# An expert layer on one core: next rows transposed earlier, bias share formed ahead, y finished by halves, four ranks counted on ScalarE, input check one expert later

## The reference

```python
N = B * S                        # 2048 tokens
k = int(CAPACITY_FACTOR * N / E) # 256 of them for each of 8 experts
xf = x.reshape(N, D)
route_prob = jax.nn.softmax(xf @ Ws + bs, axis=-1).T
route_vals, routes = jax.lax.top_k(route_prob, k)
xin = xf[routes]
h = jax.nn.gelu(jnp.einsum('ekd,edf->ekf', xin, W1) + b1[:, None, :])
out = jnp.einsum('ekf,efd->ekd', h, W2) + b2[:, None, :]
out = out * route_vals[..., None]
final = jnp.zeros((N, D), dtype=x.dtype).at[routes.reshape(-1)].add(out.reshape(-1, D))
```

## Time and profile before

| | us |
|---|---|
| median of 3 runs | 218.7 |
| the runs | 215.75, 218.7, 220.24 |
| the profiled execution, device time | 215.89 |
| its span, first to last instruction | 213.7 |

### The profile page before, as it was taken

How to read it: one execution, slowest core, us unless ns; L and a number is a source line. 1 busy time by engine, 2 the same in 40 slices (tenths; PEclk the granted TensorE clock), 3 DMA queues, 4 the chain that set the end, 5 groups by cost and what they waited for, 6 DMA issues and landing times.

```text
span 213.7 us, 3624 instructions
## 1 busy us (share of the span) xinstructions
PE 184.4 (86%) x1254; PEld 111.5 (52%) x1254; DVE 131.6 (62%) x452; ACT 88.9 (42%) x211; POOL 101.9 (48%) x111
## 2 busy tenths in 40 slices
PE   6888997997999979999999999799879878977970
PEld 2544542444433545367676766333358666865850
DVE  5787879257883898768689788888846311101120
ACT  2423772332722483135643562457535312333320
POOL 0599648000235020820247578500367787888652
PEclk9999999999999999999999999999999999999997
DMA  6625212102100001069910112100022223323123
GB/s 188 186 73 146 77 48 53 40 20 51 31 0 3 0 0 49 2 195 323 317 62 0 52 51 104 52 0 0 15 56 25 38 38 38 44 36 50 25 29 35
DMA packets 16128, 13.64 MB, mean 64 GB/s; under 512 B 3700, under 2 KB 13080, under 8 KB 16104
## 3 DMA queue, kind: packets, MB, share of 16 engines
q1 hardware_dynamic: 12246, 10.61, 16.2%
q0 software_dynamic: 2944, 2.30, 7.7%
q10 hardware_dynamic: 913, 0.43, 0.8%
HBM read 8.02 MB, written 3.21 MB: 53 GB/s over the span
## 4 chain that ended last, share of the span: by engine, by line
PE 41%; DVE 21%; POOL 15%; issue 10%; DMA 6%; ACT 3%; POOLq 1%; DVEq 0%
POOL out L1949 8%; PE psum L1014 7%; DVE mrow L1530 5%; POOL pT L1941 4%; DMA out<-pT,idx 3%; PE psum L911 3%; DVE pT L1676 3%; PE psum L1032 3%; DVE stats L1412 3%; PE psum L921 3%; PE psum L984 2%; PE psum L1095 2%; PE psum L955 2%; PE psum L1051 2%; PE psum L1083 2%
## 5 line engine op out<-in xcount | busy, mean ns | idle before, releaser
L1839 POOL TENSOR_SCALAR ve<-mv 128x4 f32<-128x4 f32 (+1 forms) x19 | 4.4, 231 | 70.3 <-DVE mv L1415 70.2
L780 ACT ACTIVATE pT<-psum 103x512 f32<-103x512 f32 (+1 forms) x36 | 21.2, 596 | 30.2 <-PE psum L986 30.2
L1949 POOL DMA_INDIRECT out<-pT,idx x16 | 25.5, 1594 | 9.7 <-issue 4.2
L911 PE MATMUL psum<-c 128*128 128x512 bf16 x108 | 27.6, 379 | 1.0 <-ACT key_map L805 1.0
L1941 POOL DMA_INDIRECT pT<-gather_rows,idx x16 | 17.7, 1103 | 21.1 <-DVE idx L1730 16.8
L1530 DVE TENSOR_REDUCE mrow<-psum 128x8 bf16<-128x616 f32 x32 | 24.6, 789 | 5.1 <-PE psum L955 5.1
L1741 DVE TENSOR_TENSOR pT<-psum,b_rows 128x256 f32<-128x256 f32 (+1 forms) x10 | 3.7, 371 | 36.2 <-PE psum L1368 36.2
L1356 PE MATMUL psum<-xinT,w 128*128 128x256 f32 (+1 forms) x80 | 16.6, 350 | 4.8 <-ACT xinT L862 4.4
L867 ACT ACTIVATE pT<-psum,b 128x256 f32<-128x256 f32 (+1 forms) x40 | 14.8, 432 | 8.1 <-PE psum L1356 8.1
L1557 DVE RECIPROCAL rden<-psum 128x512 f32<-128x512 f32 (+1 forms) x5 | 13.6, 2716 | 6.7 <-PE psum L1014 6.0
L1368 PE MATMUL psum<-w,pT 128*128 128x128 f32 x128 | 17.4, 284 | 0.2 <-DVE flag L1749 0.2
(11 more groups left out here) (198 smaller groups left out, 374.3 us busy)
## 6 DMA issues: line engine op xcount, KB each, us to landing
w<-in_L_ffn_W SPq DMA_DIRECT2D x16, 256.0 KB, 5.7
gather_rows<-xrow SPq DMA_DIRECT2D x4, 272.0 KB, 2.1
x<-in_x SPq DMA_DIRECT2D x4, 256.0 KB, 4.3
q_stack<-q_hi SPq DMA_DIRECT2D x32, 32.0 KB, 1.8
out<-res SPq DMA_DIRECT2D x4, 256.0 KB, 2.1
q_stack<-q_lo SPq DMA_DIRECT2D x24, 32.0 KB, 1.8
b_rows<-in_L_ffn_b SPq DMA_DIRECT2D x1, 512.0 KB, 3.7
pT<-gather_rows,idx POOLq DMA_INDIRECT x16, 2.6
```

The costliest lines, as they stand in the source:

```text
L780: nc.scalar.activation(pT[0:n, b % 2, s, :], ST_ps[s % 2][0:n, :], ACT.Exp).then_inc(exp_done, 1)
L911: pe.matmul(bank[b][:, :], ident16, c16[:, 0:4 * P], start=True, stop=True)
L1949: nc.gpsimd.indirect_dma_start(flat, bass.IndirectOffsetOnAxis(idx[:, h, e:e + 1], 0), y[:, e, h, :], None, bounds_check=last_row, oob_is_ ...
```

## The change

Five edits, all behind the search:
1. `EARLY = 1`: on PE the transposes of k = 1 stand ahead of y of k = 0.
2. DVE forms b2 times the route value (the bias share) in `y` as soon as the group's rows are transposed, and later, per half, one fused instruction y = psum * route value + share. `y_done` counts halves, and each scatter waits for its own.
3. ACT counts the ranks of experts 4 to 7, second half, with Sign and an accumulator. The sum of signs is mended by half the factor and by an offset in `tile_rows`, which now has a set per half. DVE counts the other four and waits for ACT ahead of the last `idx` write.
4. The check runs on DVE after k = 2, its verdict after k = 3, PE's sum ahead of y of k = 4, in bank 6.
5. A small constant, `slot_mid`, is set on DVE early in the kernel.

```diff
+EARLY = 1
-def group_of(e, h):
-    return [k for k, (of, h0, h1) in enumerate(GROUPS) if of == e and h0 <= h < h1][0]
+def halves_done(n):
+    return n // NG * E * SH + sum(h1 - h0 for _, h0, h1 in GROUPS[:n % NG + 1])
...
-    crow = (own * tile_row[:, None]).astype(np.float16)
+    signed_half = CAP // SH // 2 * J * ((np.arange(SH)[:, None] == SH - 1) & (np.arange(E)[None] >= INDEX_GROUPS[-1][0]))
+    crow = (own[:, None, :] * (tile_row[:, None, None] + signed_half[None])).astype(np.float16)
...
+                (e0, e1), h = INDEX_GROUPS[-1], SH - 1
+                act.wait_ge(idx_ps_done, (again + 1) * len(INDEX_GROUPS))
+                for e in range(e0, e1):
+                    ins = nc.scalar.activation(below[:, e - e0, :], rank_ps[-1][h][:, (e - e0) * P:(e - e0 + 1) * P], ACT.Sign,
+                                               bias=slot_mid[:], scale=-1.0, accum_out=pcount[:, h, e:e + 1])
+                ins.then_inc(act_rank_done, 1)
...
+                    if k + 1 < NG and k < EARLY:
+                        rows_T(again, k + 1)
                     if n >= 2:
-                        pe.wait_ge(y_done, n - 1)
-                    if n == 3:
+                        pe.wait_ge(y_done, halves_done(n - 2))
+                    if n == 4:
                         pe.wait_ge(suspect_done, 1)
...
-                    if k + 1 < NG:
+                    if k + 1 < NG and k >= EARLY:
                         if not again and k >= 2:
                             warm_rows(WARM, (k + 1) % 2)
                         rows_T(again, k + 1)
...
-                                for h in range(h0, h1):
+                                for h in range(h0, h1 - last):
...
+                                signs = last and h == SH - 1
+                                if signs:
+                                    dve.wait_ge(act_rank_done, again + 1)
...
                     for k, (e, h0, h1) in enumerate(GROUPS):
-                        hs, shape = slice(h0, h1), [P, h1 - h0, D]
+                        dve.wait_ge(xinT_ps_done, again * NG + k + 1)
+                        for h in range(h0, h1):
+                            ins = dve.tensor_scalar(y[:, e, h, :], b2_rows[:, e, :], xin[:, e, h, D + e:D + e + 1], None, ALU.mult)
+                        settle(ins)
                         dve.wait_ge(y_ps_done, again * NG + k + 1)
-                        settle(dve.tensor_tensor(y[:, e, hs], bank[6 + k % 2][:, h0 * P:h1 * P].rearrange("p (h d) -> p h d", d=D),
-                                                 b2_rows[:, e, :].unsqueeze(1).broadcast_to(shape), ALU.add))
-                        dve.tensor_tensor(y[:, e, hs], y[:, e, hs], xin[:, e, hs, D + e].unsqueeze(2).broadcast_to(shape),
-                                          ALU.mult).then_inc(y_done, 1)
-                        if not again and k == 1:
+                        for h in range(h0, h1):
+                            dve.scalar_tensor_tensor(y[:, e, h, :], bank[6 + k % 2][:, h * P:(h + 1) * P], xin[:, e, h, D + e:D + e + 1],
+                                                     y[:, e, h, :], ALU.mult, ALU.add).then_inc(y_done, 1)
+                        if not again and k == 2:
                             suspects()
-                        if not again and k == 2:
+                        if not again and k == 3:
                             dve.wait_ge(flag_ps_done, 1)
...
             def scatter(again, e, h):
                 n = again * E + e
-                pool.wait_ge(y_done, again * NG + group_of(e, h) + 1)
+                pool.wait_ge(y_done, n * SH + h + 1)
```

## The result

| | before | changed |
|---|---|---|
| median of 20 runs each, one chip, us | 215.81 | 215.08 |
| lowest and highest | 214.7, 223.89 | 212.95, 218.21 |
| the profiled execution, device time | 215.89 | 214.98 |
| its span | 213.7 | 213.2 |
| its granted clock, mean | 0.993 | 0.983 |

The ratio of the two kernels is 0.9933, with a 95% interval from 0.9905 to 0.9962: 1.45 us less, between 0.8 and 2.05. Both kernels have some executions several microseconds longer; the ratios here leave those out. By 2% the two kernels are the same; by the interval the changed one is the quicker. The forecast was 216.3 and within 2%.

A forecast was written before the change was run, and what follows sets the result against it. POOL, issuing indirect DMAs end to end, was taken as the bound. 1.70 at the front plus 0.64 from gathers gave 2.34 (span 213.7 to 211.4); 218.7 - 2.4 = 216.3 us against the median of three, range 213.2 to 219.2.

The forecast's parts named there:

- POOL as the bound: From 168 to 200 us POOL issues indirect DMAs end to end: 26.26 busy plus 19 gaps of 0.30.
- S(1,0): Scatter-add of expert 1, first half, on POOL: start forecast at 166.22 us in place of 167.94.
- The front, 1.70: POOL's waits for DVE at its first scatters: their removal was to gain 1.70 us by expert 1's first scatter.
- S(0,0): Scatter-add of expert 0, first half, on POOL: start forecast at 159.53 us in place of 160.03.
- S(0,1): Scatter-add of expert 0, second half, on POOL: start forecast at 161.62 us in place of 162.63.
- the moved transposes: On PE, second group's transposes during the first group's Gelu: claimed to add 0.27 us ahead of first group's y.
- ScalarE is late: Rival at the front: slow Signs delay the hidden layer to 156.95; gain 1.7 us, median 217.0; chance 0.10.
- Bias share stops POOL: Rival on DVE's bias products: 13 x 0.337 = 4.4 us lost on POOL, median 220.8; chance 0.13.
- Gathers, 0.64: Second gathers of each pair on POOL: four long ones fall to 1.06 us each, gaining 0.64 in sum.
- The end, 12.8 and rigid: From expert 6's first scatter to span end: 12.8 us set by POOL and landings alone, moving rigidly.

The follow-up runs named there:

- a_again: The changed kernel run again with no edit; median 212.36 us (6 runs), ratio 0.9884 to the kernel before.
- a_tail: The changed kernel with expert 7's first gather moved on POOL behind the scatters of expert 5; median 213.46 us, ratio 0.9871 to the kernel before.
- a_halves_undone: The changed kernel with DVE's two whole-group instructions back, no bias share ahead, y released per group; median 214.93 us, ratio 0.9931 to the kernel before.
- b_again: The kernel before run again, unaltered; median 216.39 us (10 runs), ratio 1.0011 to the kernel before.
- b_wide_rows: The kernel before with only the index constant widened to one set per half, same values; median 218.97 us (2 runs).
- a_share_x4: The changed kernel with each group's bias share formed four times instead of once; 216.48 us (1 run).

## Why the forecast held, and where its steps were off

**POOL as the bound: right.** From S(1,0) to S(5,0) POOL's 0.30 is the only idle time in the changed kernel, with 10.26 us of DVE work in 32 where there were 3.97. From S(1,0) to S(5,0) the changed kernel is 0.70 shorter than the one before (26.20 for 26.90), and the four second gathers are shorter by 0.69 in sum.

**The front, 1.70: 1.83 in a_again, 1.10 in the first profile.** Hidden layer at offset 3.46 for 3.47, S(0,0) 6.73 for 6.73, S(0,1) 8.68 for 8.82, S(1,0) 13.31 for 13.44. I had charged the moved transposes 0.27 ahead of y of k = 0; y came 2.33 after the first matmul where it had come 2.29. They fitted into PE's wait for the Gelu and cost 0.04. What the first profile lost it lost by the gap at k = 1's Gelus. The gap was in that one and in a_tail, not in the other seven kernels with `EARLY = 1` (six with ScalarE's Signs, one without). The profile names "issue" and PE, and PE and the clock look the same without the gap, so its cause is open.

**The parts don't add.** One by one, undone in the changed kernel, they cost 0.53 (transposes), 0.45 (check), 0.24 (ranks) and 0.24 (halves) at S(1,0): 1.46 for a front that gains 1.83. Each wait has POOL's sequence just below it, so some of a part's gain counts only with another.

**ScalarE is late: no.** Signs with the final read take 1.50 where I had 1.85. They are done 0.83 before the hidden layer starts.

**Bias share stops POOL: not in the changed kernel.** No scatter there is longer than before. With 64 products in place of 16 all but one kept their length, and that one lost 0.06, where this rival needed 0.18 a product. I had taken 0 from one place where DVE was held beside POOL. That came out, but not because POOL always goes first: the products happen not to run at the start of a POOL instruction with enough left, which is in part luck. The Trainium skill, page "SBUF — State Buffer", note on "DVE blocks DMA", has GpSimd unable to write its DMA descriptors while DVE runs a two-port instruction. The one scatter of 1.62 for 1.57 may be such a case; the others show no stop. Whether these products run in the mode that the note speaks of, the trace doesn't tell.

**Gathers, 0.64: 0.67 measured.** Right size and right cause, and the condition too: the prediction had the long gathers start while L1743 runs. The expectation of a_halves_undone then took it for granted that the product put back would lie on all four starts; it lay on one. The same page's section "SBUF: two separate sides", that whoever starts first keeps the ports for its whole instruction, fits the gathers that started second. It doesn't fit the other order: products with two SBUF inputs that started 0.13 to 0.44 behind a gather of 1.05 were not held. The prediction's "the trace agrees" goes for the first order alone.

**The end, 12.8 and rigid: right**, 12.87 and 12.80 (58.31 - 45.51).

**The step that failed is the base, and luck hid it.** The sum was made against the profiled execution and gave 213.5; I then set it against the median of three, 218.7, and came to 216.3. With twenty runs the same kernel has 215.81, next to the profiled 215.89: the 2.8 between the two was the chance of three draws. Without that step the forecast would have been 213.5, and too low: a base too high covered a gain too large, and that 216.3 lies only 1.2 from 215.08 is luck. The profiled execution of the changed kernel accounts for it. The experts' part is 1.78 shorter (2.34 forecast; the gap at k = 1 cost 0.73 of the 2.59 in a_again), the first gather came 1.28 later, and device time less span fell from 2.19 to 1.78: 1.78 - 1.28 + 0.41 = 0.91, the difference of 215.89 and 214.98.

The late first gather comes in either kernel, with and without the change. The clock falls short in the first part of both: b_again had 0.94 from 20 to 40 us and its first gather at 156.97. Of the changed kernel's twenty runs eight have a mean clock of 0.981 to 0.984 and spans of 212.9 to 213.6 (two more at this clock are longer, 214.6 and 216.4), six have 0.989 or more and 211.2 to 212.1. The kernel before, beside a_again, has 214.6 to 215.1 at 0.986 to 0.988, and 212.4 to 213.3 at 0.992 and over. Where both ran at 0.989 and over on that chip, the changed kernel's spans are 210.1 to 210.7, 2.4 less in the mean (210.4 against 212.8): the sum, when nothing comes between. Whether the change makes the low clock more frequent is not settled: of the kernel before's twenty runs only the times are on record. A profile with one such dip has a mean of 0.983 in the changed kernel and of 0.986 in b_again. Near these values, 0.980 to 0.984 and 0.985 to 0.988, lie 22 of 73 executions of the changed kernel and those made from it, and 19 of 61 of the kernel before and b_wide_rows.

**Open:** whether a DVE instruction with two SBUF inputs, started early enough, delays a scatter as it does a gather; what makes the gap of the Gelus, and whether it is why the quickest spans of the twenty runs (211.2) stay a microsecond above those of a_again, since one profile tells of one execution; which of the pieces common to all changed kernels (`slot_mid`, the spare tiles, one more semaphore) takes 0.4 off the time outside the span; the 0.86 behind S(7,1) in a_share_x4.

## What to carry to other kernels

Where one engine issues work end to end, count only what its own instructions gain and how long it waits ahead of its first ones; work given to the others is free up to their slack, and that slack (here 0.4 in the steady part) is the most that a reordering can win back. Compare kernels by offsets from an event that the change can't move: the first ones repeated to 0.02 here, while medians of a few runs differ by microseconds. And set a forecast against the execution whose trace it was worked out from, not against a median of three.

## What the hardware showed that I had not expected

- A gather on POOL was longer only where a DVE instruction with two SBUF inputs had started at least 0.05 ahead of it, by that instruction's remainder less about 0.13 (0.09 to 0.25 extra). One that started 0.02 ahead, or later, cost it nothing, and one with PSUM and a single SBUF input never did (0.34 and 0.26 left at the start, gathers 1.04 and 1.05).
- One scatter was longer (1.62 for 1.57) where a DVE product from SBUF to SBUF with one tensor input had started 0.10 ahead and had 0.19 left.
- Pairs of such products that start 0.38 to 0.51 into a scatter last 0.65 to 0.77, for 0.47 alone, and end 1.13 to 1.16 behind the scatter's start. Products with two SBUF inputs started 0.13 to 0.44 behind a gather's start are not held (0.42).
- Four Signs with an accumulator on ACT took 1.50 in all, one 0.37 and its read 0.21: each read lies under the start of the next Sign, and only the last one counts.
